# A convolution and sparse-coding kernel: matmuls into banks about to be overwritten, and a new order of the pieces of work

## The reference, cut to what matters

```python
x = x + conv3x3_circular(groupnorm(x), weight)        # layer 0
X = patches(groupnorm(x))                             # [1024, 1024 patches]
h_bar = h = (D.T @ X).T                               # D: normalised dictionary [1024, 512]
for k in range(1, 6):
    index = argmax(abs(h) where not chosen yet)
    ...                                               # one row of a Cholesky factor, from G = D.T @ D
    x_stack = solve(L, h_bar at the chosen atoms)
    h = h_bar - x_stack @ G[chosen]
x = x + D @ coeffs                                    # the five coefficients of each patch
```

## Time and profile before

| | us |
|---|---|
| median of three runs | 3638.73 |
| lowest and highest | 3585.6, 3663.25 |
| profiled execution, its own time | 3610.05 |
| its span, first to last instruction | 3608.2 |
| mean granted TensorE clock | 0.916 of 2.4 GHz |

### The profile page before, as it was taken

One profiled execution on the slowest core, in us unless ns is written; L12 is line 12 of the kernel. 1 busy time (PEld: TensorE's weight loads), 2 busy tenths in 40 slices (PEclk: granted clock), 3 DMA queues, 4 the chain that ended last, 5 costly groups with the idle time before them and its releaser, 6 DMA issues.

```text
span 3608.2 us, 35041 instructions
## 1 busy us (share of the span) xinstructions
PE 3072.9 (85%) x9488; PEld 1309.0 (36%) x9488; DVE 2577.4 (71%) x6596; ACT 2361.3 (65%) x3795; POOL 1915.2 (53%) x1861
## 2 busy tenths in 40 slices
PE   6796979889898999989898998989898998985446
PEld 2232334333333434333343433433343433332123
DVE  2027877768787787778777786878778786878871
ACT  3436676667867676667767676776767666665444
POOL 0015565555556565655556565665556566565651
PEclk8998989999999999989999999999999999998768
DMA  3424343533545253444535354344525443342222
GB/s 113 152 88 135 112 146 74 165 92 129 150 130 152 70 189 90 143 120 131 151 93 168 83 170 104 132 132 143 145 72 182 96 157 99 107 113 59 57 61 47
DMA packets 131028, 428.38 MB, mean 119 GB/s; under 512 B 55696, under 2 KB 55952, under 8 KB 106128
## 3 DMA queue, kind: packets, MB, share of 16 engines
q0 software_dynamic: 91136, 202.10, 23.7%
q1 hardware_dynamic: 39696, 224.05, 17.1%
HBM read 289.70 MB, written 136.31 MB: 118 GB/s over the span
## 4 chain that ended last, share of the span: by engine, by line
PE 51%; issue 11%; POOL 11%; ACT 11%; DVE 9%; DMA 5%; ACTq 0%; POOLq 0%; DVEq 0%
PE gen_ps L917 18%; PE gen_ps L908 17%; PE conv_ps L951 10%; POOL v L478 9%; PE conv_ps L958 4%; DMA u<-marked_rows,chosen 3%; ACT hot L542 3%; DVE u L831 2%; ACT score L616 2%; DVE idx L731 2%; DVE top L722 2%; POOL u L490 1%; DVE h L839 1%; ACT rb L554 1%; ACT hot L545 1%
## 5 line engine op out<-in xcount | busy, mean ns | idle before, releaser
L478 POOL DMA_INDIRECT v<-gram_rows,cell x1280 | 1288.4, 1007 | 1009.2 <-DVE cell L740 467.4
L908 PE MATMUL gen_ps<-ct,dt 128*128 128x512 f32 x2048 | 959.1, 624 | 54.3 <-ACT rb L554 36.3
L917 PE MATMUL gen_ps<-dn,z 128*128 128x512 f32 x2048 | 920.6, 603 | 45.9 <-ACT h L577 23.1
L490 POOL DMA_INDIRECT u<-marked_rows,chosen x504 | 552.3, 1096 | 511.3 <-DVE chosen L736 216.4
L951 PE MATMUL conv_ps<-xh,wc 128*128 128x512 f32 x1536 | 727.7, 625 | 76.1 <-ACT xa L584 75.1
L616 ACT ACTIVATE score<-h 128x512 f32<-128x512 f32 x640 | 380.0, 605 | 383.1 <-DVE h L839 250.1
L908 PEld LDWEIGHTS gen_ps<-ct,dt 128*128 128x128 f32 x2048 | 400.8, 200 | 568.9 <-issue 546.7
L917 PEld LDWEIGHTS gen_ps<-dn,z 128*128 128x128 f32 x2048 | 388.2, 193 | 535.3 <-issue 497.2
L722 DVE MAX8 top<-score 128x8 f32<-128x512 f32 x640 | 417.2, 690 | 212.0 <-ACT score L616 197.0
L831 DVE SCALAR_TENSOR_TENSOR u<-u,nl 128x512 f32<-128x512 f32 x748 | 515.6, 748 | 72.7 <-DMA u<-marked_rows,chosen 69.7
L951 PEld LDWEIGHTS conv_ps<-xh,wc 128*128 128x128 f32 x1536 | 301.8, 200 | 470.5 <-issue 469.3
(11 more groups left out here) (103 smaller groups left out, 1860.2 us busy)
## 6 DMA issues: line engine op xcount, KB each, us to landing
xh<-x_paired SPq DMA_DIRECT2D x128, 650.0 KB, 4.0
xa<-x_pairs SPq DMA_DIRECT2D x64, 1024.0 KB, 6.8
y_rows<-xa SPq DMA_DIRECT2D x64, 1024.0 KB, 5.1
y_rows<-rb POOLq DMA_DIRECT2D x64, 1024.0 KB, 8.5
v<-gram_rows,cell POOLq DMA_INDIRECT x1280, 2.4
u<-marked_rows,chosen POOLq DMA_INDIRECT x504, 3.9
dn<-atoms SPq DMA_DIRECT2D x1, 2048.0 KB, 7.8
gram_rows<-u SPq DMA_DIRECT2D x4, 256.0 KB, 2.0
```

Source lines behind the costliest of these rows:

```text
L478: pool.indirect_dma_start(v[:, g, k - 1, j, t:t + 1], None, cells, bass.IndirectOffsetOnAxis(ap=cell[:, g, k // (KMAX - 1), j, t:t + 1], a ...
L490: pool.indirect_dma_start(kept(img, g, k, t), None, marked, bass.IndirectOffsetOnAxis(ap=chosen[:, g, t:t + 1], axis=0))\
L908: last = pe.matmul(to[:], dt_[:, a, d, :], ct[:, a, :], start=(a == 0), stop=(a == NA - 1))
L917: last = pe.matmul(to[:], z[:, t % 2, d // PATCH, d % PATCH, :], dn[:, d, :], start=(d == 0), stop=(d == ND - 1))
```

## The change

TensorE gets a new piece, `warm`: it waits for room in a bank as the named next piece does, and then does one matmul of the dictionary (two instructions, 128 x 512) whose result nobody reads: the named piece fills the bank anew. Six stand in a period, four before `correlate 5` and one before each of `recon 0 4` and `recon 0 5`.

```diff
+            def warm(i, back, what):
+                room(i, back, what)
+                pe.matmul(gen_ps[bank_of(back, what, i == images)][:], dn[:, 0, 0:P], dn[:, 0, :], start=True, stop=True)
```

The order of TensorE's pieces in a period (W is `warm`, c convolve, k correlate, T turn, r recon; (i-1) and (i-2) left out):

```diff
- c0 k4 c1 T00 k5 T01 c2 c3 k6 T02 c4 T03 k7 r00 r01 r02 c5 r03 c6 r04 r05 r06 c7 T10 r07 average T11
-   spread T12 T13 r10 r11 r12 r13 k0 r14 r15 k1 average r16 spread r17 k2 bias k3
+ c0 k4 W c1 W T00 W c2 W T01 c3 k5 c4 k6 T02 c5 T03 k7 r00 r01 c6 r02 r03 W r04 c7 W r05 r06 r07 T10 T11
+   average T12 T13 spread r10 r11 r12 k0 average r13 k1 r14 r15 k2 r16 spread k3 r17 bias
```

`BANKS` follows that order. The plans of the other engines are new too; what the prediction speaks of:

```diff
 VECTOR_PLAN
-    1.5: [("co", 0)], 5: [("ce", 0, 0)], 8.5: [("ce", 0, 1)], 23.5: [("co", 1), ("ce", 1, 0)], 29.5: [("gn", 1, 1)],
-    30.5: [("ce", 1, 1), ("gn", 1, 2)], ... 37: [("gn", 0, 1)], 38.5: [("gn", 0, 2), ("gn", 0, 3)], 39.5: [("gn", 0, 4)],
+    1.5: [("co", 0)], 3: [("ce", 0, 0)], 10.5: [("ce", 0, 1)], 23.5: [("co", 1)], 24: [("ce", 1, 0)],
+    30: [("ce", 1, 1), ("gn", 1, 1)], ... 37: [("gn", 0, 1)], 39.5: [("gn", 0, 2), ("gn", 0, 3), ("gn", 0, 4)],
 SCALAR_PLAN
-    3: [oh001, oh011, z4, oh002, ev0, z5, oh012, oh003, oh013, oh004, oh014],
-    5: [oh021, oh031, ct00], 7: [ev1, oh022, ct01, oh032, ... oh034], 9: [ev2], 11: [z6, z7, oh101], 13: [ev3, st10, ...],
-    31: [oh122, re06, oh132, oh123, oh133, oh124, ct11, re07, oh134, ct12, ct13, rt1, z0, ...],
-    39: [re17, rt0, h2, h3],
+    0: [z4, oh001],
+    3: [ev0, oh011, oh002, oh012, oh003, oh013, oh004, oh014, ev1, z5, ct00],
+    5: [z6], 7: [ev2, oh021], 8: [oh031], 11: [oh022, ... oh034, oh101, ct01, ev3, st10, st11, st12, st0, ev4],
+    23: [st3, st14, re00, st4, re01, st5, re02, oh103, oh113, ev6, oh104, oh114, st6, re03, oh121, oh131, oh122],
+    27: [re04, ev7, re05, re06, re07, ct10],
+    31: [st16, st17, oh123, oh133, oh124, ct11, oh134, ct12, ct13, rt1, re10, z0, z1, ...],
+    39: [rt0, h3, re17],
 ADD_PLAN
-    4: [(0, 0)], 6: [(0, 1)], 7: [(1, 0)], 8: [(1, 1)],
+    4: [(0, 0)], 5: [(0, 1)], 7: [(1, 0)], 9: [(1, 1)],
```

More of the change, by code:

```diff
@@ L74 @@
 VECTOR_PLAN = {
-    1.5: [("co", 0)], 5: [("ce", 0, 0)], 8.5: [("ce", 0, 1)], 23.5: [("co", 1), ("ce", 1, 0)], 29.5: [("gn", 1, 1)],
-    30.5: [("ce", 1, 1), ("gn", 1, 2)], 31: [("gn", 1, 3)], 37: [("gn", 0, 1)], 38.5: [("gn", 0, 2), ("gn", 0, 3)],
-    39.5: [("gn", 0, 4)],
[3 rows of a table added]
 }
 SCALAR_PLAN = {
[20 rows of a table removed]
[20 rows of a table added]
 }
 ADD_PLAN = {
-    4: [(0, 0)], 6: [(0, 1)], 7: [(1, 0)], 8: [(1, 1)],
+    4: [(0, 0)], 5: [(0, 1)], 7: [(1, 0)], 9: [(1, 1)],
 }
 TAIL_VECTOR_PLAN = {
[3 rows of a table removed]
[3 rows of a table added]
 }
 TAIL_SCALAR_PLAN = {
[31 rows of a table removed]
[32 rows of a table added]
 }
 TAIL_ADD_PLAN = {
-    4: [(2, (0, 0))], 8: [(2, (0, 1))], 9: [(2, (1, 0))], 10: [(2, (1, 1))],
+    4: [(2, (0, 0))], 6: [(2, (0, 1))], 7: [(2, (1, 0))], 10: [(2, (1, 1))],
     11: [(1, (0, 0)), (1, (0, 1)), (1, (1, 0)), (1, (1, 1))],
@@ L970, in period @@
                     correlate(i, 1, 4)
+                    warm(i, 1, ("corr", 5))
                 if own:
                     convolve(i, 1)
+                if b:
+                    warm(i, 1, ("corr", 5))
                 if p:
@@ L975, in period @@
                 if b:
-                    correlate(i, 1, 5)
+                    warm(i, 1, ("corr", 5))
+                if own:
+                    convolve(i, 2)
+                if b:
+                    warm(i, 1, ("corr", 5))
                 if p:
@@ L979, in period @@
                 if own:
-                    convolve(i, 2)
                     convolve(i, 3)
+                if b:
+                    correlate(i, 1, 5)
+                if own:
+                    convolve(i, 4)
                 if b:
@@ L986, in period @@
                 if own:
-                    convolve(i, 4)
+                    convolve(i, 5)
                 if p:
@@ L994, in period @@
                     recon(i, 2, 0, 1)
[L995 to L999, removed]
                 if own:
@@ L1002, in period @@
                 if p:
+                    recon(i, 2, 0, 2)
+                    recon(i, 2, 0, 3)
+                    warm(i, 2, ("re", 0, 4))
                     recon(i, 2, 0, 4)
-                    recon(i, 2, 0, 5)
-                    recon(i, 2, 0, 6)
                 if own:
@@ L1008, in period @@
                 if p:
+                    warm(i, 2, ("re", 0, 5))
+                    recon(i, 2, 0, 5)
+                    recon(i, 2, 0, 6)
+                    recon(i, 2, 0, 7)
                     turn(i - 2, 1, 0)
-                    recon(i, 2, 0, 7)
+                    turn(i - 2, 1, 1)
                 if own:
@@ L1013, in period @@
                 if p:
-                    turn(i - 2, 1, 1)
+                    turn(i - 2, 1, 2)
+                    turn(i - 2, 1, 3)
                 if own:
@@ L1017, in period @@
                 if p:
-                    turn(i - 2, 1, 2)
-                    turn(i - 2, 1, 3)
                     recon(i, 2, 1, 0)
@@ L1022, in period @@
                     recon(i, 2, 1, 2)
+                if own:
+                    correlate(i, 0, 0)
+                if here[-1]:
+                    average(i + 1, 0)
+                if p:
                     recon(i, 2, 1, 3)
                 if own:
-                    correlate(i, 0, 0)
+                    correlate(i, 0, 1)
                 if p:
@@ L1029, in period @@
                 if own:
-                    correlate(i, 0, 1)
-                if here[-1]:
-                    average(i + 1, 0)
+                    correlate(i, 0, 2)
                 if p:
@@ L1036, in period @@
                     spread(i + 1, 0)
+                if own:
+                    correlate(i, 0, 3)
                 if p:
                     recon(i, 2, 1, 7)
-                if own:
-                    correlate(i, 0, 2)
                 if here[-1]:
                     bias(i + 1, 1 - par)
-                if own:
-                    correlate(i, 0, 3)
             def tail(i):
@@ L1048, in tail @@
                 turn(i - 2, 0, 0)
+                correlate(i, 1, 5)
                 turn(i - 2, 0, 1)
-                turn(i - 2, 0, 2)
-                correlate(i, 1, 5)
-                turn(i - 2, 0, 3)
                 correlate(i, 1, 6)
                 correlate(i, 1, 7)
+                turn(i - 2, 0, 2)
+                turn(i - 2, 0, 3)
                 recon(i, 2, 0, 0)
@@ L1061, in tail @@
                 recon(i, 2, 0, 6)
+                turn(i - 2, 1, 0)
                 recon(i, 2, 0, 7)
-                turn(i - 2, 1, 0)
                 turn(i - 2, 1, 1)
@@ L1085, in tail @@
                 recon(i, 1, 0, 6)
+                turn(i - 1, 1, 0)
                 recon(i, 1, 0, 7)
-                turn(i - 1, 1, 0)
                 turn(i - 1, 1, 1)
```

## The result

The changed kernel takes 3630.01 us (median of 19 runs, 3628.5 to 3634.5), the kernel before beside it 3617.81 (19 runs, 3585.6 to 3663.3). The ratio is 1.0061, 95% interval 1.0038 to 1.0084: slower by 0.6% (the two medians alone would give 0.3%; the ratio leaves out runs over 1.5% above the fastest of their kernel). The kernel before varies by 2% from run to run, the changed one by 0.2%. The profiled span went from 3608.2 to 3629.6 us, 21.4 more, where I had forecast 19.

A forecast was written before the change was run, and what follows sets the result against it. No engine is full; a ring of dependences sets the 204.6 us period. Terms 36.3 + 100.2 + 11.4 + 58.8 = 206.7, +2.1 a period; over 13.5 periods +28, tail -9, net +19: 3644 us against mean 3624, range 3555 to 3710.

The forecast's parts named there:

- sign of being wrong: Period below 203 us, or above 209, where a fill or wait lies on the ring instead of beside it.
- the ring: Chain of dependences through engines that sets the 204.6 us period; what lies beside it was said to cost nothing.
- S to C1: From unit 0's first score (S) to unit 1's `cell` (C1): forecast 36.3 us against 30.6, +5.7.
- X to R: From the end of unit 7's last score (X) to recon 1 0's first matmul (R): 11.4 us forecast, -1.6.
- R to S: From recon 1 0's first matmul to the next first score of unit 0: 58.8 us, no change forecast.
- C1 to X: From unit 1's `cell` to the end of unit 7's last score: forecast 100.2 us against 102.3, -2.1.
- C1 to R: From unit 1's `cell` to recon 1 0's first matmul, C1 to X and X to R together: forecast 111.6 us.
- TensorE works without a gap from convolve 4: Within C1 to X: after 3.7 us waiting for `ev3`, TensorE runs gapless through two `warm` to recon 0 7.
- slower rival: Wait for `ev3` drops the clock at convolve 4, lengthening TensorE's run: +4.5 us a period, 3704 us; chance 0.20.
- The `warm`: Six TensorE fills: four early ones free under 8.7 us of cover, the two late ones 0.87 us each.
- The rule weighed: Skill's rule that activity releases TensorE's throttle, so fills would keep the clock high; nothing of it in the sum.
- The tail: End of the program, with the last `ce(0,1)` behind the last search: 9 us gained, bounds 0 and 14.

The follow-up runs named there:

- a4: Changed kernel with ScalarE's seven `oh` of `ce(0,0)` ahead of `ev0`, and `z5`, `ct00`, `z6` behind unit 1: 3580.91 us, ratio 0.9906 to the kernel before.
- a2: Changed kernel with the two 1 MB stores of the first half issued after convolve 4 instead of convolve 3: 3561.58 us, ratio 0.9851 to the kernel before.
- c1: Changed kernel with no `warm`, late first-half stores and ScalarE's rows ahead of `ev0` together, on an ordinary chip: 3593.94 us, ratio 0.9972 to the kernel before.
- b1: Changed kernel without its four early `warm`, on a slow chip: 3912.83 us, ratio 1.0185 to the kernel before (3845.14 there).
- b3: Changed kernel with the tail's plans and TensorE order of the kernel before, on a slow chip: 3913.54 us, ratio 1.0196 to the kernel before.
- a1: Changed kernel with all six `warm` matmuls removed, order and wait for room kept: 3584.18 us, ratio 0.9917 to the kernel before.

## Why the prediction was nearly right

The time was forecast at 3644 against the mean of the runs then shown, as +19 us on the profiled execution; it is +21.4 there, and 12 between the medians. The number is right partly by luck: the loss of a full period was 3.56 us and not 2.1, and a lead of 12.3 us in the first images, which I had not looked for, hid most of that. My own sign of being wrong was a period above 209, "where some fill or wait lies on the ring"; it was 208.65, and yet one fill and one wait did lie there.

- *S to C1, 36.3.* Right to 0.2 us, and so are its parts: the first maxima at S + 3.9, `ev0` done at S + 9.1 (9.0), `chosen` at S + 19.5 (19.7), the steps of `ce(0,0)` waiting 0.61 us each. The trace shows S behind `re17` and the `oh` behind `ev0`, as forecast, and this stretch is where the kernel loses most. a4, which undoes the second, takes back 1.7 of its 5.5 us.
- *X to R and R to S.* 11.2 and 58.1 for 11.4 and 58.8.
- *C1 to X, "-2.1": the step that failed.* It is +0.6. I followed the loads behind convolve 6 away from unit 4's rows, and those did land alone (issued to 1737.39, the next gather at 1743.45 waits for nothing). But I moved only what follows convolve 6. The stores of the first half hang on `ev3` in the same way, and convolve 3 too now ends earlier against GpSimd: they came down on unit 1's rows. a2 puts the price at 5.8 us of this stretch: with late stores C1 to R is 108.3, below the 111.6 that I forecast. So a second error of 3.3 us the other way hides in the term; the wait for `ev3`, forecast at 3.7 us and found at 1.9, may be 1.8 of it, and the rest is open.
- *"TensorE works without a gap from convolve 4".* It has a gap of 4 us ahead of correlate 7, the consequence of the same miss. The wait for `ev3` is 1.9, not 3.7 us, so the slower rival's mechanism, the fall of the clock at convolve 4, did not come; it came at correlate 7.
- *The `warm`.* The two late ones cost 1.74 us as priced. The four early ones were said to be free as long as they hide ahead of T12. One of them does not: it holds `ev1`, which I had written into the path of S to C1 myself (`z6` behind `ev1`) without putting the `warm` ahead of it on TensorE. It costs 0.6 to 0.8 us. The rest of what the six cost is the shifted fall of the clock.
- *The rule weighed.* By the Trainium skill ("TensorE: Matmul & The Clock Gate", Part 1) activity releases the throttle. These traces agree in the main: with a `warm` inside the gap, 2.50 us ahead of convolve 1, its twelve instructions take 5.40 us in every period of a4; without it, behind 3.37, they take 6.8 to 8.4 in ten of eleven periods of c1 and 5.40 in one. The period's long stretch at half clock, at the turns of group 1, is as before (0.53 against 0.51); no `warm` stands in it.
- *The tail, -9.* 5.5 less from the last full period on; b1 and b3 differ by 13.5 there on a slow chip. The bounds 0 to 14 hold both.
- *The start.* I multiplied the period's +2.1 by 13.5 and looked at no other. The steady loss is 3.56 in eleven periods; the 12.3 us of lead from the first images hid two thirds of that error. Where the lead comes from was not tried.

## What to carry to other kernels

A piece that moves takes with it every transfer that hangs on its semaphore, on whichever queue: list them all, and look what each now meets. In an order that is a ring, filling idle time on an engine is free only if nothing behind the fill releases another engine's work; follow each fill to the next signal. And a fill that holds the clock in one gap may only lengthen the next one: ask where the engine will be idle instead. Two edits that each gain alone may draw on the same slack; look what each hides behind before adding them.

## What the runs showed of the hardware that I had not expected

- Four indirect gathers of rows issued together with two 1 MB stores landed about 3 us later than alone: 6.4 to 7.6 us after issue, against 3.5 to 3.7 with the stores 5.6 us behind the last gather. With the stores 4.0 us ahead of the first gather it was 6.5 to 7.1 (a2, unit 2), with them 1.3 us ahead 10.4 to 11.7 (c1, unit 2); in these two a 650 KB and a 1 MB load went out just before the stores. VectorE's wait for the first was 4.96 against 0.59 us.
- The clock behind a wait is not settled by the length of the wait: behind 2.8 us without `warm` twelve instructions took 5.40 us in two of eleven periods and 6.8 to 8.5 in the others (a1), behind 3.4 us 5.40 in one and 6.8 to 8.4 in ten (c1). Behind 1.9 us, or behind 2.5 with a `warm` ahead, they took 5.40 in all.
- Of the four chips of the experiments two ran this program 6% slower (3845 and 3857 us for the kernel before, against 3623 on both others), with the long stalls shown above. The order of the kernels was another one there: late stores in the kernel before were best, at 0.9945 and 0.993.
